# Last layer: the second softplus sum between the score maxima, half of the decays ahead of the query's copy

## What is computed

```python
# mixing branch
dt = softplus(x_dbl[..., :64] @ dt_proj_w + dt_proj_b)
delta = softplus(dt + dt_proj_b)                    # the second softplus
state = exp(delta * A) * state + (delta * u) * B    # 256 positions, 16 states: "decays" are exp(delta * A)
y = (state @ C + u * D) * silu(z);  s = y @ out_proj_w.T
# gate
scores = q @ k.T / sqrt(8);  attn = softmax(scores);  x1 = layernorm(x + (attn @ v) @ Wo + bo)
g = layernorm(x1 + sum_e comb_e * expert_e(x1))
x = x + s * silu(g)
```

## Time and profile before

| | us |
|---|---|
| median of 3 runs (lowest, highest) | 3066.57 (3063.77, 3068.05) |
| the profiled execution, its own time | 3067.96 |
| its span, first to last instruction | 3065.1 |
| first maxima of the last layer to its last, 17 sets | 1648.2 to 3040.4 |

### The profile page before, as it was taken

One profiled execution on the slowest core, in us unless ns is written; L12 is line 12 of the kernel. 1 busy time (PEld: TensorE's weight loads), 2 busy tenths in 40 slices (PEclk: granted clock), 3 DMA queues, 4 the chain that ended last, 5 costly groups with the idle time before them and its releaser, 6 DMA issues. The chain is left out here.

```text
span 3065.1 us, 55428 instructions
## 1 busy us (share of the span) xinstructions
PE 2518.5 (82%) x18804; PEld 1909.3 (62%) x18804; DVE 2332.1 (76%) x6047; ACT 1725.6 (56%) x3461; POOL 323.5 (11%) x356
## 2 busy tenths in 40 slices
PE   1777777779999999977746888888888889888886
PEld 1555555557777777765544666666666666656665
DVE  2777777768888888867426888888888888888887
ACT  1666666656565556644334555656656556656554
POOL 0000000000000000003230111111111111111111
PEclk9989988989999999989875877777777777777777
DMA  7000000000000000020112334433333434433334
GB/s 212 1 0 0 0 0 0 0 1 1 1 0 1 0 1 0 1 74 14 40 54 63 94 90 104 104 86 81 84 90 91 104 91 104 99 82 84 83 88 113
DMA packets 86514, 163.66 MB, mean 53 GB/s; under 512 B 18856, under 2 KB 45616, under 8 KB 86320
## 3 DMA queue, kind: packets, MB, share of 16 engines
q0 software_dynamic: 20480, 62.93, 10.8%
q1 hardware_dynamic: 64640, 98.15, 9.9%
q10 hardware_dynamic: 1200, 0.27, 0.1%
HBM read 92.60 MB, written 9.99 MB: 33 GB/s over the span
## 5 line engine op out<-in xcount | busy, mean ns | idle before, releaser
L1124 ACT ACTIVATE b_neg<-b_neg,b_nmax 128x128 f32<-128x128 f32 (+1 forms) x512 | 190.9, 444 | 213.1 <-DVE b_nmax L1278 213.1
L2527 ACT ACTIVATE d_probs<-l_bank,w_b 128x256 f32<-128x256 f32 x512 | 210.7, 469 | 155.7 <-PE l_bank L2365 153.3
L2790 DVE TENSOR_TENSOR_SCAN d_state<-w,d_state 128x1024 f32<-128x1024 f32 x128 | 291.0, 2284 | 3.7 <-issue 3.3
L2365 PE MATMUL l_bank<-xnT,w_w 128*128 128x256 f32 x1024 | 245.1, 382 | 13.7 <-ACT d_probs L2527 13.7
L2376 PE MATMUL l_bank<-w_w,d_probs 128*128 128x128 f32 x2048 | 252.7, 276 | 0.0
L2376 PEld LDWEIGHTS l_bank<-w_w,d_probs 128*128 128x128 f32 x2048 | 244.9, 192 | 11.7 <-ACT d_probs L2527 5.3
L2295 PE MATMUL l_bank<-w 9*128 9x256 f32 x1040 | 208.7, 669 | 26.4 <-ACT w L2450 18.9
L94 POOL TENSOR_TENSOR ln_rstd<-ln_var_eps,minus_half 128x2 f32<-128x2 f32 x50 | 64.0, 1279 | 1503.3 <-DVE ln_var_eps L88 1503.3
L2489 ACT ACTIVATE w<-d_delta,d_negA 128x255 f32<-128x255 f32 x520 | 220.2, 499 | 0.0
L2365 PEld LDWEIGHTS l_bank<-xnT,w_w 128*128 128x128 f32 x1024 | 184.7, 190 | 40.4 <-ACT d_probs L2527 20.6
L2295 PEld LDWEIGHTS l_bank<-w 9*128 9x128 f32 x1040 | 123.5, 319 | 97.1 <-issue 31.5
(11 more groups left out here) (405 smaller groups left out, 5759.0 us busy)
## 6 DMA issues: line engine op xcount, KB each, us to landing
d_bct<-l_bc SPq DMA_DIRECT2D x132, 512.0 KB, 3.9
d_state<-d_state POOLq DMA_DIRECT2D x96, 512.0 KB, 6.5
d_state<-d_state POOLq DMA_DIRECT2D x32, 256.0 KB, 4.1
x_sorted<-x SPq DMA_DIRECT2D x1, 2560.0 KB, 16.6
w<-in_L_ffn_w_dram SPq DMA_DIRECT2D x1, 2048.0 KB, 9.5
w_w<-in_L_ffn_W_dram SPq DMA_DIRECT2D x1, 2048.0 KB
c2e_xg<-x_sorted SPq DMA_DIRECT2D x16, 128.0 KB
y_sorted<-c2e_yo SPq DMA_DIRECT2D x16, 128.0 KB, 1.8
```

Source lines behind the costliest of these rows:

```text
L1124: done = nc.scalar.activation(neg[:, slot, cols], neg[:, slot, cols], ACT.Exp, bias=nmax[:, slot, a:a + 1], scale=-1.0)
L2365: done = nc.tensor.matmul(bank[:, b, i * T:(i + 1) * T], w.w1[:, e, k * P:(k + 1) * P], x1T[:, :], start=True, stop=True)
L2527: done = v.activation(hid[:, e % 2, k, :], bank[:, b, i * T:(i + 1) * T], ACT.Gelu, bias=w.b1[:, e, k:k + 1])
L2790: done = v.tensor_tensor_scan(group, dA[i][:, g % (NG - 1), :, :].rearrange("p m t -> p (m t)"), group, 0.0, ALU.mult, ALU.add)
```

## The change

On DVE the second softplus sum leaves `third_part` and stands between the first and the second maximum of the same sequence. On ACT the decays of state groups 0 and 1 (16 instructions) leave the exponentials and stand between the second `log_part` and the query's copy. Those of groups 2 and 3 stay with the exponentials, but only behind pairs 1, 3, 5 and 7. It holds for the prologue (sequence 0) and for every `n + 1` in the loop.

```diff
                 v.activation(probs[:, p % PS, :, :], back[:, 2 * (p % 2):2 * (p % 2) + 2, :], ACT.Exp,
                              scale=float(HD3) ** -0.5).then_inc(probs_ready, 1)
-                decays(n, p // 2, p % 2)
+                if p % 2:
+                    decays(n, 2 + p // 4, p // 2 % 2)
...
                     log_part(n + 1, 0)
                     copy_qk(n + 1)
                     log_part(n + 1, 1)
+                    for k in range(4):
+                        decays(n + 1, k // 2, k % 2)
                     copy_qm(n + 1)
...
             def third_part(m, par):
-                softplus_sum(m, 1)
                 v.tensor_tensor(du[:, :, :], delta[:, :, :], xs[:, par, :, :], ALU.mult)
...
                     for blk in range(NBLK):
                         heads_max(n + 1, blk)
+                        if blk == 0:
+                            softplus_sum(n + 1, 1)
                     third_part(n + 1, 1 - par)
```

More of the change, by code:

```diff
@@ L2513, in _ @@
             log_part(0, 1)
+            for k in range(4):
+                decays(0, k // 2, k % 2)
             copy_qm(0)
@@ L2777, in _ @@
                 heads_max(0, blk)
+                if blk == 0:
+                    softplus_sum(0, 1)
             third_part(0, 0)
```

## The result

The changed kernel takes 3073.17 us (median of 11 runs, 3070.64 to 3074.98) against 3065.22 us of the kernel before in 11 runs (3063.77 to 3068.05): a ratio of 1.0025, 95% interval 1.0016 to 1.0035. It is slower by 0.25%, where 3073.0 us had been forecast.

A forecast was written before the change was run, and what follows sets the result against it. PE's order was taken to bound the attention stretch behind the maxima, not ACT's queue. 15 x 0.56 - 1.15 - 0.86 = +6.4 us on the 3066.57 median gave 3073.0 us, range 3066.5 to 3078.5.

The forecast's parts named there:

- The chain: From L2304 on, PE's own order (pair, head output, pair) sets the pace; its 31.0 us of pauses are exponential latency.
- The sum's place: Sum between maxima 0 and 1: later maxima 0.73 us late, turned outputs and L2824 0.56 late, 8.4 us in all.
- The 0.17 us that L2304 gives back: L2304 no longer waits for ym, so 0.17 of the 0.73 us delay is absorbed.
- Loop edges: After every fourth sequence: PE's 2.16 us gap moves with L2304, so the edges pay 0.56 us too; otherwise 1.7 less.
- The rival that let the edges absorb the delay: Three loop edges take no delay and the clock's surplus falls: +2.7 us, 3069.3; 32%, with lesser forms.
- the four forecast terms: Steady sequences and loop edges 15 x 0.56 us, first sequence -1.15, behind the last sequence -0.86; sum +6.4 us.
- the base of 3066.57: Median of the runs shown of the kernel before, to which the sum was added for 3073.0 us.
- First sequence and tail: ACT's shorter queue frees PE in the first sequence, -1.15 us once; earlier ACT copy behind the last sequence, -0.86 once.
- The decays are hidden: Sixteen decays on ACT end before the query's copy, with 2.5 us of cover, 2.1 in the worse count.
- The clock: PE's half clock from maxima to turned outputs; recovery behind L2824 varies, surplus 3.1 us over 15 lengths, ±2 us.
- The rival of ACT's relief: PE's 31.0 us of waits for probabilities are ACT's queue, so relief gains -21.8 us: 3044.8 us; 8%.

The follow-up runs named there:

- the relief alone: Kernel before with the decays of state groups 0 and 1 cut from 255 to 8 columns; 3063.24 us, ratio 0.9990.
- the sum alone: Changed kernel with all decays back behind the exponentials, the second softplus sum still between maxima 0 and 1; 3078.17 us, ratio 1.0043.
- PE's order: Transpose of the next input moved behind pair 7 in three kernels: before 3051.32 us, changed 3051.81, second sum on GpSimd and ACT 3041.12.
- the kernel before with the move: Kernel before with PE's transpose of the next normed input moved from between score pairs 5 and 6 to behind pair 7; 3051.32 us, ratio 0.9946.

## Why the prediction was right, point by point

- **The chain.** Shown by the relief alone (39.65 unchanged, pauses 1.10 and 1.12), by the sum alone (40.33 with ACT's queue as before), and by PE's order (-1.03 a sequence in the kernel before).
- **The sum's place, 0.56 us a steady sequence.** The mechanism held; the term was too small. It measured 0.69. The maxima came 0.86 late instead of 0.73. Of that, 0.08 is the sum with its drain, which takes 0.85 us between the maxima and not the 0.77 that was read where `du` follows (2176.40 to 2177.18). Another 0.03 is the pitch: before, the first two maxima start 2.21 us apart, and the 2.24 of the prediction is the mean of three unlike pitches (2.21, 2.29, 2.20). The 0.17 us that L2304 gives back is there in full (0.86 - 0.69).
- **Loop edges.** Charged with 0.56 each, they cost -0.05 in the mean. PE's gap there fell from 2.16, 1.99 and 2.22 us to 1.20, 1.63 and 1.30, in all by 2.24 us, against 3 x 0.69 = 2.07 of delay. The rival that let the edges absorb the delay was right in this part. The two errors, +1.6 over 12 sequences and -1.8 over three, cancel by luck: the four forecast terms sum to +6.3 in the traces, against +6.4. It is also luck that 3073.0 lies within 0.2 us of 3073.17: the base of 3066.57 was 1.35 above the median of 11 runs, and the measured difference of 7.95 was 1.55 above the forecast 6.4.
- **First sequence and tail.** -1.15 and -0.86 had been forecast, -1.07 and -0.74 came; most of the difference is the later maxima again (0.79 us late in the first sequence, 0.86 at the tail, where 0.73 had been set).
- **The decays are hidden.** 2.52 us of cover were left, 2.5 had been worked out, and no maximum got longer.
- **The clock.** PE is at 0.50 in the attention stretch (line below), as in the earlier trace rows, and the stretches from the reciprocal to the next maximum sum to 743.3 us against 743.8. The prediction speaks of 15 such lengths; its 3.1 us of surplus belong to all 16. The rule of the Trainium skill ("TensorE: Matmul & The Clock Gate", Part 1) that idleness throttles had no price of its own here, the half clock lying over this stretch already.

```profile
2189.00:2206.00 17.00, 14.78 (x98) 6.89 (x90) 15.28 (x16) 10.41 (x19) 2.65 (x1) 0.50 0.08 29
```

- **The rival of ACT's relief.** The advice of "Perfetto Trace Analysis", Optimization Strategies, in the Trainium skill, is to "optimize those engines that are blocking the critical path". The table of waits alone doesn't tell which those are. It names ACT, but PE's waits for it are 31.9 us with ACT relieved and 34.7 in the relief alone, against 31.0, and 35.5 in the kernel before with the move, which is 18.7 us faster. Followed one step further, the chain leads to PE's own order, and with that the advice holds here.

What stays open is the loop edge. The step of a sequence behind an edge exceeds a steady one's by 1.7 to 2.3 us in the three kernels in which L2304 still waits for `ym` (before, the relief alone, before with the move), and by 1.1 to 1.7 in the other eight. So the edge costs less where that wait is gone; no run took the wait away by itself, and the cause isn't shown.

## What to carry to other kernels

Moving an operation to where its result is wanted sooner also puts it ahead of whatever the same engine owes others: here 0.68 us of DVE work went in front of three maxima on which the matmul engine hung, to feed an engine that had time. When a table says that A waits for B, look whether B itself was waiting for A a moment earlier; if it was, the pause is a latency, and only A's order, or work put into the pause, removes it. An idle engine can be the better place for the piece: with the sum on GpSimd and ACT the maxima took 8.99 us, as before, and the decays were still done 1.54 us before the query's copy.

## What the runs showed of the hardware that was not expected

- The same sum and drain have no fixed price. From the sum's start to the next maximum it is 0.85 us in the loop, with 0.17 of "issue", and 0.60 without the drain. In the prologue it is 0.78, and for the second sum 0.83, both without an idle time shown; at every fourth place that second sum is followed by 0.52 us of "issue".
- Two score pairs that the kernel puts on different row groups of TensorE overlap fully: 16 records take 2.10 us, eight take 2.08. An operation on all 128 rows, queued between two such pairs, cost 1.43 us in the changed kernel against its own 0.69 (start of pair 5 to head output 2: 4.63 us with it, 2194.75 to 2199.38, and 3.20 without).
- The idle time at a loop edge is not a constant of the loop. PE's is 1.6 to 2.2 us in the three kernels in which L2304 waits for `ym`, and 0.9 to 1.6 in the other eight. At the edge behind 2008.82 us in the changed kernel PE stands idle for 1.20 us, ACT for 2.13 and DVE for 3.22, all charged to "issue"; in the kernel before, where ACT was still busy with decays, ACT shows no such gap there.
